# Weight parts stored burst by burst, part 1 loaded twice, x loads behind the stores

## The reference, cut to what matters

```
masked_w = weight * mask[None, :, :]
w_bot = jnp.einsum('bg,got->bot', y, masked_w)
return x + jnp.einsum('bnt,bot->bno', x, w_bot) + bias
```

## Time and profile before

| | |
|---|---|
| three runs, us | 647.01, 640.91, 646.6 |
| profiled execution, us | 643.54 |
| its span (first to last instruction), us | 641.1 |
| time around the span, us | 2.4 |
| TensorE matmul busy | 629.0 us, 98% |
| VectorE busy | 411.7 us, 64% |
| ScalarE busy | 297.0 us, 46% |
| GpSimd busy | 110.2 us, 17% |
| granted TensorE clock, mean | 0.997 of full speed |
| HBM read, written | 97.10 MB, 46.14 MB |

### The profile page before, as it was taken

One profiled execution on the slowest core, in us unless ns is written; L12 is line 12 of the kernel. 1 busy time (PEld: TensorE's weight loads), 2 busy tenths in 40 slices (PEclk: granted clock), 3 DMA queues, 4 the chain that ended last, 5 costly groups with the idle time before them and its releaser, 6 DMA issues.

```text
span 641.1 us, 18487 instructions
## 1 busy us (share of the span) xinstructions
PE 629.0 (98%) x7808; PEld 594.3 (93%) x7808; DVE 411.7 (64%) x425; ACT 297.0 (46%) x513; POOL 110.2 (17%) x95
## 2 busy tenths in 40 slices
PE   6999999999999899999999999999999999999997
PEld 2466779999999899999999999999999999999997
DVE  4986777556655567766776667666676676667421
ACT  0131226666666354445545545455445544554500
POOL 4594586353431000000000000000000000000000
PEclk9999999999999989999999999999999999999999
DMA  8959979999989796455599984555599985652112
GB/s 319 398 176 358 323 219 295 304 330 308 294 278 329 249 292 198 136 162 153 150 271 299 316 236 139 150 155 160 137 238 316 320 248 141 169 150 97 51 67 82
DMA packets 63649, 144.44 MB, mean 225 GB/s; under 512 B 8078, under 2 KB 33776, under 8 KB 53360
## 3 DMA queue, kind: packets, MB, share of 16 engines
q1 hardware_dynamic: 44624, 109.34, 58.0%
q10 hardware_dynamic: 18944, 33.93, 15.6%
HBM read 97.10 MB, written 46.14 MB: 223 GB/s over the span
## 4 chain that ended last, share of the span: by engine, by line
PE 93%; DMA 3%; DVE 2%; issue 1%; ACT 1%; SPq 0%; ACTq 0%; DVEq 0%
PE ps L568 70%; PE ps L549 15%; PE ps L529 7%; DMA w_parts<-parts 2%; DVE wbot L465 1%; DVE raw L449 1%; ACT wbot L406 1%; DMA first_sb<-in_first 1%; DMA ring<-w_parts 1%; DVE ring L457 0%; DVE yblk L484 0%; DVE staged L478 0%; SPq L301 0%; SPq L286 0%; DVE ring L455 0%
## 5 line engine op out<-in xcount | busy, mean ns | idle before, releaser
L568 PE MATMUL ps<-wbot,xs 128*128 128x128 f32 x4096 | 478.2, 277 | 0.8 <-DVE wbot L465 0.4
L568 PEld LDWEIGHTS ps<-wbot,xs 128*128 128x128 f32 x4096 | 466.0, 193 | 5.5 <-issue 4.7
L406 ACT ACTIVATE wbot<-ps 128x512 f32<-128x512 f32 x448 | 259.5, 610 | 224.2 <-PE ps L568 115.8
L478 DVE TENSOR_TENSOR staged<-ps,bias_sb 128x512 f32<-128x512 f32 x128 | 88.5, 691 | 197.8 <-PE ps L568 197.6
L455 DVE COPY ring<-ring 32x4096 bf16<-32x4096 bf16 x112 | 137.2, 1225 | 7.3 <-DMA ring<-w_parts 3.9
L549 PE MATMUL ps<-ydiag,ring 98*128 98x64 bf16 x3584 | 117.2, 193 | 2.8 <-DVE ring L457 2.5
L549 PEld LDWEIGHTS ps<-ydiag,ring 98*128 98x128 bf16 x3584 | 114.8, 98 | 4.3 <-issue 2.6
L457 DVE COPY ring<-ring 16x4096 bf16<-16x4096 bf16 x88 | 107.2, 1218 | 2.7
L365 POOL TENSOR_TENSOR raw<-raw,parts 128x512 f32<-128x512 f32 x32 | 45.7, 1428 | 68.9 <-ACT parts L397 68.8
L465 DVE TENSOR_TENSOR wbot<-ps,ring 128x512 f32<-128x512 f32 x64 | 43.1, 687 | 14.1 <-PE ps L529 10.4
L397 ACT ACTIVATE parts<-raw 128x512 bf16<-128x512 f32 x32 | 19.7, 623 | 50.4 <-DVE raw L449 33.3
(11 more groups left out here) (10 smaller groups left out, 4.0 us busy)
## 6 DMA issues: line engine op xcount, KB each, us to landing
xs<-in_x SPq DMA_DIRECT2D x32, 1024.0 KB, 12.0
out<-staged ACTq DMA_DIRECT2D x128, 256.0 KB, 4.0
ring<-w_parts SPq DMA_DIRECT2D x112, 256.0 KB, 5.7
ring<-w_parts SPq DMA_DIRECT2D x136, 128.0 KB, 6.6
w_parts<-parts SPq DMA_DIRECT2D x32, 384.0 KB, 9.3
raw<-in_w SPq DMA_DIRECT2D x16, 512.0 KB, 9.3
ring<-in_w SPq DMA_DIRECT2D x4, 512.0 KB, 14.9
ring<-in_eye SPq DMA_DIRECT2D x112, 16.0 KB
```

The costliest lines, as they stand in the source:

```text
L406: eng.activation(chunk_place(b, k), chunk_sums(b, k), ACT.Copy).then_inc(s_ev_a, 1)
L478: eng.tensor_tensor(staged[:, n % OUTB, :].rearrange("p (b o) -> p b o", b=GB), ps2[n % S2B][:, :].rearrange("p (b o) -> p b o", b=GB), bi ...
L568: ins = eng.matmul(ps2[n % S2B][:, b * SL:(b + 1) * SL], xs[:, load % GROUPS * GB + b, k, :], at, start=(k == 0), stop=(k == KT - 1))
```

## The change

The change has five parts.

1. *Layout of the scratch tensor.* Before, it was ordered by half, part, weight matrix and output; a burst's 32 rows of 8 KB lay 32 KB apart. Now it is ordered by half, burst, part (w2, w1, w3), row: the 32 rows of one load lie one behind the other, and a store writes runs of 1 KB (512 values, `TW`) where it wrote runs of 512 B. The raw weights and the mask come in the new order from the host; the mask tile is twice as large (256 KB in place of 128 KB, eight times).
2. *Ring loads.* For every burst, two loads of 32 rows: w2 and w1 into rows 0 to 31, and w1 and w3 into rows 64 to 95. `thrice` goes, and with it the third load of the first 24 bursts.
3. *VectorE.* One copy for each burst; the second copy (L457) is gone.
4. *The order on SyncE.* Within a step the stores of parts stand ahead of the x loads. The x loads of a quarter, which began one step behind the last use of the quarter's first place, begin two steps behind it (`X_AT`).
5. *Tiles.* Tiles 16 to 31 stand 1.25 steps apart in place of 1.4: the last one at step 26 in place of 29. The small tensor `yblk` moves into a slot of the ring that is still free then.

```diff
+CH = CS // 2
-TW = 256
-HCOLS = P // OJ * TW
+TW = 512
+PART1, PART2, PART3 = 1, 0, 2
-            **{8 + (t - 16) * 7 // 5: (t,) for t in range(16, TILES)}}
+            **{8 + (t - 16) * 5 // 4: (t,) for t in range(16, TILES)}}
-X_AT = {_g: LAST_USE[_g - _g % GROUPS - GROUPS] + 1 + _g % GROUPS * 9 // 7 for _g in range(GROUPS, XLOADS)}
+X_AT = {_g: LAST_USE[_g - _g % GROUPS - GROUPS] + 2 + (_g % GROUPS * 4 + 1) // 3 for _g in range(GROUPS, XLOADS)}
-def thrice(b):
-    return b < FB + 3 * CS
...
             def store_parts(t):
-                at = scratch[h, 0, i, 0, :]
-                to = bass.AP(tensor=at.tensor, offset=at.offset, ap=[[TW, P], [ROWS // TG * HCOLS, 3 * TG], [1, TW]])
+                at = scratch[h, 0, 0, i * TG * OJ, :]
+                to = bass.AP(tensor=at.tensor, offset=at.offset, ap=[[TW, P // CH], [3 * ROWS * BW, CH], [ROWS * BW, 3], [1, TW]])
...
             def load_burst(b):
-                eng.dma_start(ring[0:2 * ROWS, i, :], w1_w2).then_inc(s_w12[i], 16)
-                eng.dma_start(ring[5 * ROWS:KROWS, i, :], w3).then_inc(s_w3[i], 16)
-                if thrice(b):
-                    w1 = scratch[h, 0, :, :, c % KT * BW:(c % KT + 1) * BW].rearrange("g o c -> (g o) c")
-                    eng.dma_start(ring[4 * ROWS:5 * ROWS, i, :], w1).then_inc(s_w1[i], 16)
+                w21 = scratch[h, c % CH, 0:2, :, :].rearrange("j r c -> (j r) c")
+                w13 = scratch[h, c % CH, 1:3, :, :].rearrange("j r c -> (j r) c")
+                eng.dma_start(ring[0:2 * ROWS, i, :], w21).then_inc(s_w21[i], 16)
+                eng.dma_start(ring[4 * ROWS:KROWS, i, :], w13).then_inc(s_w13[i], 16)
...
+                for t in TILES_AT.get(n - 2, ()):
+                    store_parts(t)
                 for g in range(GROUPS, XLOADS):
                     if X_AT[g] == n:
                         load_x(g)
-                for t in TILES_AT.get(n - 2, ()):
-                    store_parts(t)
...
             def duplicate(b):
                 eng.tensor_copy(ring[2 * ROWS:4 * ROWS, i, :], ring[0:2 * ROWS, i, :]).then_inc(s_dup, 1)
-                if not thrice(b):
-                    eng.tensor_copy(ring[4 * ROWS:5 * ROWS, i, :], ring[0:ROWS, i, :]).then_inc(s_dup, 1)
...
-    scratch = nc.dram_tensor("w_parts", (HALVES, 3, NG, OJ, HCOLS), mybir.dt.bfloat16, kind="Internal").ap()
+    scratch = nc.dram_tensor("w_parts", (HALVES, CH, 3, ROWS, BW), mybir.dt.bfloat16, kind="Internal").ap()
```

More of the change, by code:

```diff
@@ L123, in on_vector @@
     return b < FB
-COPIES = [0] * (FB + 1)
-for _b in range(FB, BURSTS):
-    COPIES.append(COPIES[-1] + (1 if thrice(_b) else 2))
 V_DONE, A_DONE = [0], [0]
@@ L156, in cond_resid_kernel @@
         staged = sb("staged", [P, OUTB, BANK], fp32)
-        raw = sb("raw", [P, RAWN, TG, TW], fp32)
-        parts = sb("parts", [P, PARTN, 3, TG, TW], bf16)
+        raw = sb("raw", [P, RAWN, TW], fp32)
+        parts = sb("parts", [P, PARTN, 3, TW], bf16)
         mask_sb = sb("mask_sb", [P, 2, TW], fp32)
@@ L166, in cond_resid_kernel @@
         pick_sb = sb("pick_sb", [KALL, 3 + OJ], fp32)
-        yblk = sb("yblk", [P, BANK], fp32)
         raw01_sb = [xs[:, RAW0:RAW0 + CS, :, :].rearrange("p c k n -> p c (k n)"),
                     ring[:, 2:4, :].rearrange("p i c -> p (i c)").bitcast(fp32).rearrange("p (c t) -> p c t", c=CS)]
+        yblk = ring[:, 1, BW // 2:BW // 2 + 2 * BANK].bitcast(fp32)
         mask_t_sb = ring[:, 1, 0:2 * KT * FU * SL].bitcast(fp32).rearrange("p (k o) -> p k o", k=KT)
@@ L196, in cond_resid_kernel @@
         s_store = [sem(f"s_store{i}") for i in range(PARTN)]
-        s_w12 = [sem(f"s_w12_{i}") for i in range(RING)]
-        s_w3 = [sem(f"s_w3_{i}") for i in range(RING)]
-        s_w1 = [sem(f"s_w1_{i}") for i in range(RING)]
+        s_w21 = [sem(f"s_w21_{i}") for i in range(RING)]
+        s_w13 = [sem(f"s_w13_{i}") for i in range(RING)]
         s_eye = [sem(f"s_eye{i}") for i in range(RING)]
@@ L212, in high_half @@
         def high_half(t):
-            return raw[:, t % RAWN, :, :].rearrange("p g c -> p (g c)").bitcast(bf16) \
-                .rearrange("p (g c h) -> p g c h", g=TG, h=2)[:, :, :, 1]
+            return raw[:, t % RAWN, :].bitcast(bf16).rearrange("p (c h) -> p c h", h=2)[:, :, 1]
         def stored(eng, t):
@@ L255, in load_raw @@
                 at = t % RAWN
-                eng.dma_start(raw[:, at:at + 2, :, :], w[t // 2]).then_inc(s_raw[at // 2], 16)
+                eng.dma_start(raw[:, at:at + 2, :], w[t // 2]).then_inc(s_raw[at // 2], 16)
             def load_first(u, c, count):
@@ L362, in subtract @@
             def subtract(t):
-                at, w1 = raw[:, t % RAWN, :, :], parts[:, t % PARTN, 0, :, :]
+                at, w1 = raw[:, t % RAWN, :], parts[:, t % PARTN, PART1, :]
                 eng.wait_ge(s_p1, t + 1)
@@ L396, in cast_w1 @@
                     stored(eng, t - PARTN)
-                eng.activation(parts[:, t % PARTN, 0, :, :], raw[:, t % RAWN, :, :], ACT.Copy).then_inc(s_p1, 1)
+                eng.activation(parts[:, t % PARTN, PART1, :], raw[:, t % RAWN, :], ACT.Copy).then_inc(s_p1, 1)
             def cast_w2(t):
                 eng.wait_ge(s_rest, t + 1)
-                eng.activation(parts[:, t % PARTN, 1, :, :], high_half(t), ACT.Copy).then_inc(s_p2, 1)
+                eng.activation(parts[:, t % PARTN, PART2, :], high_half(t), ACT.Copy).then_inc(s_p2, 1)
             def evict(b, k):
@@ L528, in first_burst @@
                     room(b, k)
-                    ins = eng.matmul(ps1[(b * KT + k) % S1B][:, :], raw01_sb[u][:, c, k * P:(k + 1) * P], yblk[:, :],
+                    ins = eng.matmul(ps1[(b * KT + k) % S1B][:, :], raw01_sb[u][:, c, k * P:(k + 1) * P], yblk,
                                      start=True, stop=True)
```

33 lines of the change are left out of this document (14 added, 19 removed).

## The result

The changed kernel is **slower**: 658.69 us median of four runs (656.8 to 661.0) against 646.23 us for the kernel before, ratio **1.0212**, 95% interval 1.0149 to 1.0276; whether it is slower by 2%, four runs leave open. The forecast was 640.4 us, with a range up to 649. What came true is a rival of the prediction, x loads as the new stall, which it priced at 658 us for 0.9 us per enlarged load. That the total is so near is in part luck: the rival put waits of 5.5, 5.5 and 2.9 us into quarters 2, 3 and 4, and the trace has 8.2, 3.2 and 3.0.

What follows compares the result with a forecast made beforehand. The prediction took TensorE's matmuls, busy 98% of the span, as the bound, with one mid-run stall at burst 44. Its sum was 643.5 - 4.1 (stall) + 1.0 (late x load 22) = 640.4 us, range 637 to 649.

Steps and rivals of the forecast that it cites:

- x loads as the new stall: Rival: late x loads make PE wait, 646.6 us at price 0.55, 658 at 0.9; chance 0.25 below 653 us, 0.09 above.
- Burst 44: Mid-run stall: PE waits 2.46 us because tile 31's store is late; an earlier store was to remove the wait.
- the 4.1 us go: Burst 44's whole stall, 2.46 us idle plus slower clock behind it, counted as a gain of 4.1 us.
- the rows do not tell … I take nothing: Quarter 2's x loads: lateness costed at nothing, with quarter 3's sum as the other bound.
- what is late next: After the stall: ScalarE's wait for the store of tile t-5, some 18 us of cover against 16.6, costed at nothing.
- I take 0.45, by bytes: Price in us of 128 KB more per late burst's ring load in the full queue, at 294 GB/s.
- The upper bound, 0.9: Highest price in us of the extra 128 KB: a whole load of 256 KB by the full queue's rate.
- two rules: Trainium skill on the larger ring load: by ports reached it takes no longer; by disjoint halves serializing, its bytes count.
- The later x steps: Quarter 3: x loads issued later; with larger ring loads, load 22 lands 1.0 us late, load 23 just in time.
- No clock loss: Quarter 3: the 1.0 us wait for load 22 was taken to leave the clock at 2.4 GHz.
- What was costed at nothing: Second copy, 1 KB store runs, mask tile, ScalarE's store wait and first 24 bursts: no cost or gain on PE.
- The scatter of the runs: If runs differ by the stall's length, the changed kernel's lie close to the sum; otherwise up to 3 us above.

Runs made afterwards that it cites:

- Experiments 1 and 8: Kernel before with stores ahead of x loads; experiment 1 also has tiles 1.25 steps apart: 642.52 us (ratio 0.999) and 642.86 us (0.9974).
- experiment 6, e_rows32: Changed kernel with w1 and w3 loaded into rows 32 to 63 and VectorE copying to rows 64 to 95: 680.67 us, ratio 1.0473.
- e_order_late: Kernel before with stores ahead of x loads, tiles 1.25 steps apart and the changed kernel's later x steps: 644.76 us, ratio 1.0016.
- experiment 4: Changed kernel with x loads at their old, earlier steps: 646.92 us, ratio 1.0032; run again for its profile, 646.13 us.
- e_copy: Changed kernel with the old ring loads: w3 alone in rows 80 to 95, w1 copied by VectorE after burst 40: 644.84 us, ratio 1.0013.
- e_after_early2: Changed kernel with x loads at their old, earlier steps, run again for its profile: 646.13 us.
- e_order: Kernel before with only stores ahead of x loads and tiles 1.25 steps apart: 642.52 us, ratio 0.999.
- e_first36: Kernel before with stores ahead of x loads, tiles 1.25 and x loads one step apart, third load ended four bursts earlier: 640.09 us, ratio 0.9942.
- Experiment 5, e_split: Changed kernel with the load into rows 64 to 95 issued as two loads of 16 rows: 663.6 us, ratio 1.0303.
- e_dve32: Kernel before with stores ahead of x loads, tiles 1.25 steps apart, VectorE's third copy from burst 32 instead of 40: 642.73 us, ratio 0.9982.

## Why the prediction was wrong

**Burst 44: right, and worth next to nothing.** The store left when the prediction said (187.12 for "about 187") and landed before 204, and the wait is gone in every kernel that has the store moved. But "the 4.1 us go" was the first step that failed, in the sentence on quarter 2: "the rows do not tell … I take nothing". The trace of the kernel before did tell: load 15 had 0.8 us to spare, and a PE that comes 2.5 us earlier, or more with the clock, finds it missing. Experiments 1 and 8 show that wait, 3.61 and 2.56 us, with no larger load in the kernel. With the larger loads and the later steps the second quarter lost 8.2 us, more than half of the 14.4, where the forecast had nothing. The question "what is late next" was asked of ScalarE alone.

**The price of 128 KB: the step that failed in size.** "I take 0.45, by bytes", from the stretch's mean of 294 GB/s. It was 0.89 us by the landings and 0.83 to 0.99 by load 22's margin. The upper bound, 0.9, was written down, and by it the rival gave 658. A figure nearer than the mean was in the same trace: the 256 KB ring load took 1.37 us behind its neighbour in the kernel before, 187 KB/us, where an x load ran at 1024 / 4.04 = 253; by it 128 KB cost 0.68. The mean of a stretch that is mostly x loads is not the rate of a ring load. Nor does a mean show a tail: for thirteen of load 22's sixteen completions the forecast's price was about right (0.37 us), and the group waits for the last.

The prediction weighed this against two rules. Rows 0 to 31 and 64 to 95 took 1.59 and 1.53 us where the load of 16 rows took 0.64, so the larger load did take longer. The Trainium skill, SBUF — State Buffer, Door 1: The DMA port swizzle, from which the prediction read that it would not, fails in that reading. Another is not shown, but fits the time of experiment 6, where it mattered which rows are written. By the same section of the Trainium skill, rows 32 to 63 lie on the ports of rows 0 to 31, and rows 64 to 95 on the others. The two ring loads of a burst took turns, 3.12 us together. By the Trainium skill, DMA: Bandwidth & Descriptors, Rules for kernel authors, transfers to different halves serialize; on that the trace agrees.

**The later x steps: too dear.** Load 22's margin without larger loads was to shrink from 11.5 to 3.5 us; it was 6.7 in e_order_late, so the steps cost 4.7 us, not 8.0. This error had the other sign and hid part of the price's: 11.4 - 4.7 = 6.7 us of margin, and the larger loads took 9.9 to leave -3.2, where the forecast was 11.5 - 8.0 - 4.5 = -1.0. With both errors the forecast came nearer than with the price's alone. In quarter 4 the same sum was to leave load 30 with 1.6 us; it had 6.3 in e_order_late and was 2.96 late in the changed kernel.

**"No clock loss": the waits that came were longer.** It hung on a wait of 1.0 us. Waits of 5.32, 3.21 and 2.96 us were each followed by a stretch at 1.2 GHz; a wait of 1.25 us (experiment 4) was not. With the stall's 4.1 us gone, 14.4 us of waits and 3.9 + 1.6 us of clock (1.6 being what the stall had lost behind it) the sum would have been 643.5 - 4.1 + 14.4 + 5.5 = 659.3; the profiled execution took 658.6.

**What was costed at nothing.** The second copy, the stores in runs of 1 KB, the mask tile and ScalarE's wait for stores: no wait of PE in the changed kernel names them, and e_copy stands where e_order_late does. These held. So did the first 24 bursts, though x loads 11 to 13, which follow them, had 2.1, 0.6 and 0 us to spare where the kernel before had 12.1, 12.6 and 14.8. With the new loads at the old steps (e_after_early2) they had 11.1, 5.2 and 2.6, no less than the 8.4, 5.2 and 2.8 of e_order; with the old loads at the later steps (e_order_late) 2.6, 1.9 and 0. So the order and the later steps took that margin.

**The scatter of the runs.** The prediction left open whether the kernel before scatters by the length of its stall. e_first36, which has no wait over 1.1 us behind the start in its trace, hardly scatters, which suggests that waits of this kind are most of it.

**The trade itself.** The change took from VectorE, which had room, 107 us that PE waited for at burst 44 alone, and gave SyncE's queue, which had none in three stretches, 88 x 128 KB.

**Open.** Why a few of the sixteen completions fall behind the others while the queue is full, by 7.3 us at load 22, and whether they are always the same ones; and by what path rows 32 to 63 cost more. Experiment 5 rules out the number of rows in one load, and experiment 6 shows the place, but no more.

## What to carry to other kernels

A stall that is removed is a gain only if what PE needs next is early enough. Before counting it, list the spare time of every transfer that the same queue lands in that stretch, and compare the smallest with the time saved: here 0.8 us against 4.1. Price more bytes in a full queue by the landing-to-landing time of the same kind of transfer, not by the stretch's mean rate, and check it against the steps of what lies behind it. And where a queue is full, changing the order moves the wait; fewer bytes take it away, and four bursts' worth (e_first36) were enough.

## What the runs showed of the hardware

- **Clock and idle time.** Waits of 1.08, 1.25 and 1.31 us left the clock at 1.00. Waits of 2.46, 2.56, 2.96, 3.21, 3.61 and 5.32 us were followed by a stretch at 1.2 GHz, and so were 1.78 us in e_dve32 (0.82 behind it) and 2.08 in e_split (0.84). But 2.87 us in the changed kernel was not: the window 228.50 to 234.20 behind it has 1.00. Nor were 2.41 and 2.12 in e_rows32 (257.60 to 274.00). Length alone does not decide.
- **Issue is a wait too.** With the DMA share at 1.04 (e_order, 180 to 189 us) an issue on SyncE takes 5.75 us (an x load at 182.74) where most take 0.4 to 0.6, and everything behind it in the list is late.
- **Splitting did not help.** Two loads of 16 rows in place of one of 32 gave 663.6 us for 658.69; the intervals of the two ratios overlap.
- **A landing has a tail.** The last of load 22's sixteen completions came 7.3 us behind the thirteenth in the changed kernel, 1.2 us in e_order_late.
- **The layout in HBM cost no time.** The kernel took the same whether the 8 KB rows of a load lay 32 KB apart or one behind the other (644.76 and 644.84 us).
